# Last tile's router weights and eight ring loads moved to GpSimd in a fused cross-attention and mixture-of-experts block

## The reference

```
x = x + tanh(g_xattn) * attention(layernorm(x), ctx)        # 16 heads of 8
t = layernorm(x)
probs = sigmoid(t @ router_w.T + expert_bias)               # [1792, 160]
top_w, top_idx = top_k(probs, 8)
top_w = 2.5 * top_w / (sum(top_w) + 1e-9)
combine = zeros(1792, 160); combine[token, top_idx] = top_w
h = silu(t @ w_gate[e].T)                                   # for every expert e
routed = sum over e of (h * combine[:, e]) @ w_down[e].T
x = x + tanh(g_ffn) * (routed + shared expert)
```

## Time and profile before

| | |
|---|---|
| median of three runs | 1124.95 us (1122.03 to 1126.83) |
| the profiled execution | 1124.83 us, its span 1123.2 us |
| TensorE busy | 1068.0 us, 95% |
| VectorE busy | 963.5 us, 86% |
| ScalarE busy | 847.6 us, 75% |
| GpSimd busy | 591.7 us, 53% |
| ring, 900 to 1100 us | TensorE 200.00 of 200 us busy, DMA engines 77%, 232 GB/s |

### The profile page before, as it was taken

One profiled execution on the slowest core, in us unless ns is written; L12 is line 12 of the kernel. 1 busy time (PEld: TensorE's weight loads), 2 busy tenths in 40 slices (PEclk: granted clock), 3 DMA queues, 4 the chain that ended last, 5 costly groups with the idle time before them and its releaser, 6 DMA issues.

```text
span 1123.2 us, 37415 instructions
## 1 busy us (share of the span) xinstructions
PE 1068.0 (95%) x12142; PEld 708.1 (63%) x12142; DVE 963.5 (86%) x1699; ACT 847.6 (75%) x1817; POOL 591.7 (53%) x984
## 2 busy tenths in 40 slices
PE   2799999999999999999999999998999999999998
PEld 1366777777777777777777777654455555555554
DVE  4678888888888888888888888578999999999998
ACT  3476777777777777777777776687888888888887
POOL 5798887887888888788888886320000000000000
PEclk9799999999999999999999999999999999999999
DMA  8778777577577576676676652482788778777873
GB/s 159 158 166 214 145 178 179 123 184 170 133 186 170 131 186 162 142 185 152 152 185 142 150 132 67 110 207 97 229 228 226 226 236 237 229 229 227 230 237 118
DMA packets 229501, 197.12 MB, mean 175 GB/s; under 512 B 161039, under 2 KB 207263, under 8 KB 229462
## 3 DMA queue, kind: packets, MB, share of 16 engines
q1 hardware_dynamic: 218036, 173.22, 61.8%
q0 software_dynamic: 9200, 21.85, 6.9%
q10 hardware_dynamic: 2226, 1.56, 0.7%
HBM read 109.96 MB, written 12.55 MB: 109 GB/s over the span
## 4 chain that ended last, share of the span: by engine, by line
PE 75%; DVE 12%; issue 4%; SPq 3%; ACT 2%; DMA 2%; DVEq 0%; POOL 0%; ACTq 0%
PE bank L1550 15%; PE bank L1540 15%; PE bank L1343 12%; PE bank L1377 11%; PE bank L1358 10%; DVE part_max L1030 6%; PE bank L1413 5%; PE bank L1401 4%; DVE rec L1169 2%; PE bank L1457 1%; SPq L369 1%; DMA ctx_in<-in_ctx_dram 1%; SPq L405 1%; DVE o_raw L1044 1%; DVE kparts L1160 1%
## 5 line engine op out<-in xcount | busy, mean ns | idle before, releaser
L800 ACT ACTIVATE p_exp<-bank 125x448 f32<-125x448 f32 x768 | 400.1, 544 | 183.9 <-PE bank L1358 182.9
L1030 DVE TENSOR_REDUCE part_max<-bank 128x1 f32<-128x500 f32 x672 | 420.1, 671 | 62.0 <-PE bank L1377 61.5
L1358 PE MATMUL bank<-q_st,k_stk 97*125 97x224 f16 x1536 | 272.6, 261 | 2.5 <-ACT p_exp L800 1.9
L1377 PE MATMUL bank<-kparts,q_blk 128*128 128x500 f16 x672 | 255.8, 384 | 17.5 <-DVE part_max L1030 13.2
L1358 PEld LDWEIGHTS bank<-q_st,k_stk 97*125 97x125 f16 x1536 | 195.9, 138 | 66.2 <-ACT p_exp L800 13.1
L867 ACT ACTIVATE ctT<-bank 128x448 f32<-128x448 f32 x320 | 174.2, 545 | 40.9 <-DVE v_sb L1203 9.8
L1210 DVE TENSOR_TENSOR ctT<-v_sb,ctT 128x448 f16<-128x448 f32 (+1 forms) x324 | 200.4, 619 | 0.2
L1550 PE MATMUL bank<-ctT,w_ring 128*128 128x448 f16 x816 | 198.9, 352 | 0.1
L874 ACT ACTIVATE ctT<-v_sb 128x448 f16<-128x448 f32 x320 | 182.2, 569 | 7.0 <-DVE v_sb L1203 6.9
L1343 PE MATMUL bank<-p_exp,v_sb 125*25 125x168 f32 (+1 forms) x6144 | 186.2, 262 | 0.4 <-ACT p_exp L800 0.4
L1343 PEld LDWEIGHTS bank<-p_exp,v_sb 125*25 125x25 f32 x6144 | 142.1, 103 | 42.6 <-ACT p_exp L800 0.5
(11 more groups left out here) (193 smaller groups left out, 1376.3 us busy)
## 6 DMA issues: line engine op xcount, KB each, us to landing
k_stk<-kparts SPq DMA_DIRECT2D x384, 93.8 KB, 4.1
v_sb<-c_scratch SPq DMA_DIRECT2D x68, 448.0 KB, 4.3
k_stk<-c_scratch SPq DMA_DIRECT2D x68, 448.0 KB, 4.3
ctx_in<-in_ctx_dram SPq DMA_DIRECT2D x30, 672.0 KB
w_scratch<-w_out POOLq DMA_DIRECT2D x80, 128.0 KB, 3.2
w_in<-in_L_ffn_w_gate_dram POOLq DMA_DIRECT2D x80, 64.0 KB, 3.7
w_in<-in_L_ffn_w_down_dram POOLq DMA_DIRECT2D x80, 64.0 KB, 4.1
v_sb<-c_scratch SPq DMA_DIRECT2D x8, 336.0 KB, 3.8
```

The costliest lines, as they stand in the source:

```text
L800: act.activation(p_exp[0:KP, j % PR, f * 448:(f + 1) * 448], ST[f][0:KP, 0:448], ACT.Exp).then_inc(exp_done, 1)
L1030: v.reduce_max(part_max[:, i // NCH, i % NCH:i % NCH + 1], SM[i % NSM][:, 0:CK], axis=AX.X).then_inc(sm_maxed, 1)
L1358: last = pe.matmul(ST[f][0:KP, (g % 2) * GC:(g % 2 + 1) * GC], k_stk[0:97, u, g, j * KP:(j + 1) * KP], q_st[0:97, u, g, :, :].rearrange("p ...
L1377: pe.matmul(SM[i % NSM][:, 0:CK], rows, kparts[:, u, 0, c * CK:(c + 1) * CK], start=True, stop=True).then_inc(sm_done, 1)
```

## The change

The two operations of `late_weights` leave VectorE. GpSimd does them as `weights(TS)`, the function that now also makes the other tiles' weights, behind `late_shift()`. The eight loads of the ring rows of pairs 12 to 15 leave SyncE's list and stand at the end of GpSimd's. They wait there for the store of the last tile (`c_stored[TS]`) and, pair by pair, for `h_done`, as they did on SyncE. They have semaphores of their own, `c_ahead`; the counts that the loop waits for are lowered by the 32 that these loads no longer add. No instruction is added to the loops.

```diff
+        c_ahead = [sem(f"c_ahead{i}") for i in range(WR)]
...
+        def weights_of(eng, n, q, here, t1=NTC):
+            for a in range(2):
+                src = c_scratch[n:n + 1, a, 0:t1 * TC] if isinstance(n, int) else \
+                    c_scratch[bass.ds(n, 1)].rearrange("o a t -> o (a t)")[:, a * N:(a + 1) * N]
+                eng.dma_start(c_ring[q][a::2, 0:t1, :],
+                              src.rearrange("o (t c) -> o t c", c=TC).to_broadcast([I, t1, TC])).then_inc(here, 16)
...
@@ block.sync
-            for n in range(AHEAD, AHEAD + WR):
-                sp.wait_ge(h_done, TS * (n - WR) + TS)
-                weights_of(n, n % WR)
...
-                    weights_of(i * WR + q, q)
+                    weights_of(sp, i * WR + q, q, c_here[q])
@@ block.gpsimd
-            for c in range(TS):
+            def weights(c):
                 p = slice(c * PPC, (c + 1) * PPC)
                 pool.wait_ge(top_done, 2 * PPC * (c + 1))
                 then(pool.tensor_tensor(comb[:, p, :], prob[:, p, :], comb[:, p, :], ALU.subtract))
                 pool.wait_ge(sums_done, c + 1)
                 pool.tensor_tensor(comb[:, p, :], comb[:, p, :], wsum[:, 2, p].unsqueeze(2).to_broadcast([PT, PPC, E]),
                                    ALU.mult).then_inc(comb_done, 1)
+
+            for c in range(TS):
+                weights(c)
...
             late_shift()
+            weights(TS)
+            pool.wait_ge(c_stored[TS], 16)
+            for n in range(AHEAD, AHEAD + WR):
+                pool.wait_ge(h_done, TS * (n - WR) + TS)
+                weights_of(pool, n, n % WR, c_ahead[n % WR])
@@ block.vector
-            def late_weights(part):
...
-                    if k == TOP_LATE + 3:
-                        late_weights(0)
-                    if k == TOP_LATE + 4:
-                        late_weights(1)
...
-                        if t == 0:
-                            dve.wait_ge(c_here[q], i * 32)
+                        if t == 0 and first:
+                            dve.wait_ge(c_ahead[q], 32)
+                        elif t == 0:
+                            dve.wait_ge(c_here[q], i * 32 - 32)
```

More of the change, by code:

```diff
@@ L455, in _ @@
             attention(sp, body, B - 2, first=2)
[L458 to L463, removed]
             for c in range(NCH):
@@ L489, in _ @@
                 sp.wait_ge(h_done, TS * (n - WR) + TS)
-                weights_of(n, n % WR, TS)
+                weights_of(sp, n, n % WR, c_here[n % WR], TS)
             sp.wait_ge(cb_cp, 2 * NTC)
@@ L1251, in pairs @@
                         k = i * (WR * NTC) + (q * NTC + NTC + t)
-                        if t == 0:
-                            dve.wait_ge(c_here[q], i * 32)
+                        if t == 0 and first:
+                            dve.wait_ge(c_ahead[q], 32)
+                        elif t == 0:
+                            dve.wait_ge(c_here[q], i * 32 - 32)
                         weigh(k, t, k - (NTC - 1), c_ring[q][:, t, :])
                         lo_part(k - 1, (t - 1) % NTC)
-            pairs(AHEAD // WR)
+            pairs(AHEAD // WR, True)
             with dve.Fori(AHEAD // WR + 1, EP // WR) as i:
```

## The result

The changed kernel took 1132.13 us (median of five runs, 1129.22 to 1133.76) beside 1124.95 for the kernel before (1122.03 to 1127.24): a ratio of 1.0071, 95% interval 1.0049 to 1.0093. Its profiled run took 1133.76 us with a span of 1132.2, against 1124.83 and 1123.2: 9.0 us more.

A forecast was written before the change was run, and what follows sets the result against it. TensorE, busy 95% of the span, was taken as the bound. Gains of 1.46 and 1.42 us (-2.88) plus a 4.7 us load price gave +1.8 us on 1124.83, about 1126.7; range 1121.5 to 1130.4.

The forecast's parts named there:

- Part 1: Last tile's weights moved from VectorE to GpSimd: TensorE keeps its pace around them, a gain of 1.46 us.
- the 1.6 of cover: Slack between GpSimd finishing the late weights, by 774.7, and TensorE transposing them at 776.3: some 1.6 us.
- GpSimd makes the weights late: Rival: GpSimd's pair needs over 1.6 us more than the rows give; time about 1124 us, chance 0.04.
- The price of the loads: Late tile: GpSimd's eight loads share the DMA engines with SyncE's rows, costing 4.7 us (1.8 to 7.4).
- turns by packets: Main case: both DMA queues alternate packet by packet while loaded, delaying the late tile's rows; 1123.7 to 1129.3 us, chance 0.53.
- pair 5: Late tile's rows of pair 5 land at 802.0, wanted at 797.2: 4.9 us late at 319 GB/s.
- 0.2 off: Taken from the late tile's 4.9 us because VectorE's wait of 1.62 us cost TensorE 1.42; leaves 4.7.
- Part 2's gain: Ring's start: with eight loads issued early by GpSimd, VectorE's 1.62 us wait goes, gaining 1.42 us on TensorE.
- hide: Rival: GpSimd's loads fit beside the late tile's, VectorE waits under 2 us; 1121.9 to 1123.7 us, chance 0.24.
- go first: Rival: GpSimd's ring rows take nearly all the engines, first late pair 6.7 us late; 1128.4 to 1130.6 us, chance 0.12.
- over 10: Byte ratio of GpSimd's queue to SyncE's, instead of 2.5, if packets held some 9 to 17 descriptors.

The follow-up runs named there:

- The writes in the same place: Kernel before with the weights on GpSimd, its two operations replaced by memsets of the same 112x640 elements, loads on SyncE: 1121.89 us, one run.
- Part 2 alone: Changed kernel with the last tile's weights back on VectorE, the eight ring loads still on GpSimd: 1130.4 us, ratio 1.0051 to before.
- Part 1 alone: Changed kernel with the eight ring loads back on SyncE, the last tile's weights still on GpSimd: 1125.75 us, ratio 1.0015 to before.

## Why the prediction was wrong

It said 1126.7 us, at most 1130.4; 1132.13 lies above the range. In the profiled spans the sum was +1.8 and is +7.5, a miss of 5.7 us, in two steps.

**The failed step is Part 1: the time of GpSimd's pair in its new place.** "GpSimd's pair of the same operations takes 1538 + 1253 ns in its three earlier uses" is true of those, but most of their neighbours on VectorE were of other kinds. One such use in after, and VectorE beside it:

```profile
717.47 1.54 POOL L693 TENSOR_TENSOR ctx_in<-kparts,ctx_in 112x640 f32<-112x640 f32 x1 [2.70 <-DVE ctx_in L1126]
```

```profile
717.30 1.00 DVE L1119 MAX8 top<-kparts 112x8 f32<-112x160 f32 x4
718.33 0.19 DVE L1132 TENSOR_REDUCE wsum<-top 112x4 f32<-112x32 f32 x1
718.55 0.48 DVE L1133 TENSOR_SCALAR wsum<-wsum 112x4 f32<-112x4 f32 x1
...
722.96 0.64 DVE L1179 TENSOR_TENSOR o_nrm<-rec,o_raw 128x224 f32<-128x224 f32 x1
```

The first two have one operand in SBUF and take their usual time. `o_nrm` has two, and it starts while GpSimd's third product runs (722.11 to 723.36): it takes 0.64 us, its median is 0.39, and GpSimd keeps its 1.25. So the place was not free even there, for VectorE, and before's trace has the same two durations, 0.64 and 0.48. In the new place the neighbours are multiplies and subtractions with two SBUF operands, one after the other. GpSimd took 5.59 + 1.51 us and was done 7.3 us behind the end of the last replacement, not 3.0. Of these 4.3 us the 1.6 of cover hide their part, which leaves 2.7, and the stop is 2.6.

-1.46 was forecast, +2.72 came: 4.2 us of the miss. Of these, 2.78 are the transposes, which start that much later than forecast, and 1.40 are TensorE's clock at 0.50 behind the stop, for which the prediction has no term. The 1.34 + 1.05 us for which GpSimd held two of VectorE's operations cost nothing here, since TensorE stood still meanwhile; in the ring such a hold is what costs. The writes in the same place gave exactly -1.46, so VectorE's side of the step was right, and only the price of the place was missing. "GpSimd makes the weights late" was among the rivals, with 0.04, since three like uses seemed to exclude it, and for Part 1 it came true; its time, "about 1124", was too low, because it has neither the low clock nor Part 2's price. The rule that would have raised it stands in the Trainium skill (SBUF — State Buffer, "Who interferes with whom") and was not weighed.

**The price of the loads was mis-sized.** The mechanism was right: turns by packets, nothing at the first pair, then waits up to the sixth ("pair 5"), in the forecast and in the rows alike. The term was 4.7 us and is 6.3 in after (7.4 in Part 2 alone), the rest of the miss. Two sizes were off. "Turn by turn, GpSimd's queue would take 2.5 bytes for one": in 790 to 800 it took 2.46 against 0.79 MB, 3.1 to one, from 590 and 545 packets of 4.2 and 1.45 KB. In the records of single packets 431 of q0's 511 data packets hold three rows of 1792 bytes and 80 one, and all 443 of q1's hold one; the others are 4 bytes. The late tile got 79 GB/s, not 91, and a pair took 2.9 us, not 2.51. So the sixth pair is 5.9 us behind before's pace, where 4.7 was forecast (4.9 less the "0.2 off", for which no run shows a reason). The other 0.4 us of the stretch is again the clock, which the sum leaves out. Issue by GpSimd was faster than forecast, 0.61 to 0.64 us in place of 747 ns, which changes nothing.

**Part 2's gain was right**: 1.42 on TensorE from a wait of 1.62; the segment is 1.65 us shorter in every kernel that asks early for these rows. Of the ways in which the loads could go all but one are out: from 1.84 MB on they don't hide, they don't go first, they take turns. The 9 to 17 descriptors in a packet that the Trainium skill gives (DMA: Bandwidth & Descriptors, "Queues, rings and completion order") are not what the packets of this trace show: three rows on one queue, one on the other. The "over 10" of the prediction would also need packets that long on GpSimd's queue alone.

Four things stay open. The first is why VectorE lets GpSimd in at 777.46 and not before. No gap of VectorE's shows there, in after or in Part 1 alone, where it is again the ninth operation. The second is why `TENSOR_SCALAR`, with one operand, took 0.48 us beside GpSimd at 718.55, where its median is 0.17: no run varies VectorE's side. The third is what makes the clock fall. One stop of 2.61 or 4.12 us came before a fall, and so did four shorter ones in a row in after's late tile; before's single stop of 1.26 us and the two of 0.80 and 0.18 us with two pairs on GpSimd did not. No run was made to find out. The fourth is the first column of the table, which varies by up to 5 us between kernels that don't differ there.

## What to carry to other kernels

A duration belongs to its neighbours: before an operation is moved to GpSimd, look at what VectorE does at that moment, not only at what GpSimd needed elsewhere. If VectorE runs operations with two SBUF operands back to back and is on or near the path, a reading operation on GpSimd costs both engines; here a write didn't, and neither did a product on ScalarE. If the moved work makes TensorE stand, look at the granted clock behind the stop: here it cost another 1.4 us on a stop of 2.6. If transfers are late because their issuer has too many of them, make fewer and larger ones in the same queue, which keeps their order; a second queue brings them forward at the cost of whatever the first one is carrying, by the ratio of packet sizes.

## What was not expected of the hardware

- VectorE kept a reading operation of GpSimd out for eight of its own, 4 us, and was then held for 1.34 us by it; in the ring, with gaps of some 0.06 us in a step, GpSimd's operation took 1.79 us, and the VectorE operation that began 0.44 us behind it took 1.83.
- After a stop of TensorE of 2.61 us its granted clock was 0.50 from 781.9 to 785.1, and after one of 4.12 us it was 0.51 from 809.1 to 815.8; the steps took up to 2.24 us for 1.136.
- Of two queues with work, GpSimd's moved three bytes for one of SyncE's when both copied rows of 1792 bytes: about as many packets, three rows in most of its own.
- A load of SyncE's with 128 rows takes 0.64 us to issue, as long as one with 64.
- A megabyte on the second queue was free while the first had 3.2 us of slack at its start; the next 2.75 MB cost 7.4 us, 1.2 of them by the low clock.
